# Products that nobody reads in the waits at the seams, key transposes spread over a run-up, and a reordered entry of a feed-forward

## The reference

```
x = x + tanh(g_xattn[l]) * attention_l(layernorm(x), ctx)
x = x + tanh(g_ffn[l])   * feed_forward_l(layernorm(x))
```

## Time and profile before

| | |
|---|---|
| median of the runs | 1395.36 us (3 runs, 1392.48 to 1397.9) |
| the profiled execution | 1396.31 us, of which its span is 1394.3 us |
| TensorE busy | 1329.4 us, 95% of the span |
| VectorE busy | 921.2 us, 66% |
| ScalarE busy | 604.1 us, 43% |
| GpSimd busy | 502.3 us, 36% |
| mean granted TensorE clock | 0.981 |

### The profile page before, as it was taken

How to read it: one execution, slowest core, us unless ns; L and a number is a source line. 1 busy time by engine, 2 the same in 40 slices (tenths; PEclk the granted TensorE clock), 3 DMA queues, 4 the chain that set the end, 5 groups by cost and what they waited for, 6 DMA issues and landing times.

```text
span 1394.3 us, 21141 instructions
## 1 busy us (share of the span) xinstructions
PE 1329.4 (95%) x8191; PEld 1081.1 (78%) x8191; DVE 921.2 (66%) x1352; ACT 604.1 (43%) x1046; POOL 502.3 (36%) x364
## 2 busy tenths in 40 slices
PE   6999999999999999998999999999899999899987
PEld 5989888988889889987798888889785444477733
DVE  5588778864588778875557774587756774343277
ACT  3444444443344444442244443344335778222252
POOL 5126435371126646415312543124343000243212
PEclk9999999999999999999999999999997999999989
DMA  5111111121011121020121112012104000462000
GB/s 189 54 54 50 47 52 56 31 72 39 16 54 50 46 72 42 16 94 20 27 63 55 48 37 68 22 30 61 31 1 132 2 1 2 140 156 73 1 0 31
DMA packets 55105, 70.94 MB, mean 51 GB/s; under 512 B 26672, under 2 KB 32976, under 8 KB 55008
## 3 DMA queue, kind: packets, MB, share of 16 engines
q1 hardware_dynamic: 55008, 69.60, 16.8%
HBM read 57.13 MB, written 5.37 MB: 45 GB/s over the span
## 4 chain that ended last, share of the span: by engine, by line
PE 85%; DVE 9%; ACT 3%; issue 2%; DMA 0%; POOL 0%; SPq 0%; DVEq 0%; ACTq 0%
PE ps L771 13%; PE ps L746 12%; PE ps L720 9%; PE ps L755 9%; PE ps L713 8%; PE ps L705 5%; PE ps L1709 4%; PE ps L690 4%; PE ps L1313 3%; PE ps L1339 3%; PE ps L1722 2%; PE ps L1295 1%; PE ps L1324 1%; PE ps L1414 1%; PE ps L1032 1%
## 5 line engine op out<-in xcount | busy, mean ns | idle before, releaser
L847 ACT ACTIVATE pT<-ps 128x768 fp32r<-128x768 f32 x192 | 156.0, 813 | 290.9 <-PE ps L755 289.6
L771 PE MATMUL ps<-pT,vv 128*128 128x256 f32 (+1 forms) x1728 | 251.3, 290 | 2.5 <-DVE oT L957 2.5
L950 DVE TENSOR_TENSOR pT<-ps,pT 128x768 fp32r<-128x768 f32 x192 | 183.7, 957 | 78.5 <-ACT pT L847 77.9
L746 PEld LDWEIGHTS ps<-kT,qT 128*128 128x128 f32 (+1 forms) x1152 | 201.2, 188 | 41.6 <-DVE qT L902 1.9
L746 PE MATMUL ps<-kT,qT 128*128 128x512 f32 (+3 forms) x1152 | 231.4, 336 | 1.5 <-DVE qT L902 1.5
L771 PEld LDWEIGHTS ps<-pT,vv 128*128 128x128 f32 (+1 forms) x1728 | 215.2, 180 | 3.1 <-DVE pT L950 2.9
L855 ACT ACTIVATE prob<-ps,rows_and_turned 128x768 f32<-128x768 f32 x192 | 172.5, 898 | 77.9 <-DVE rows_and_turned L938 77.9
L938 DVE TENSOR_REDUCE rows_and_turned<-ps 128x1 f32<-128x768 f32 x192 | 182.7, 951 | 24.8 <-PE ps L746 24.5
L630 POOL TENSOR_TENSOR wo<-raw,one 128x512 fp32r<-128x512 f32 (+1 forms) x48 | 50.0, 1041 | 409.9 <-PE ps L720 407.8
L720 PE MATMUL ps<-wo,oT 128*128 128x512 f32 (+1 forms) x576 | 169.0, 402 | 5.1 <-DVE x L892 2.4
L755 PE MATMUL ps<-ident,prob 128*128 128x128 f32 x1152 | 157.3, 272 | 3.0 <-DVE pT L950 3.0
(11 more groups left out here) (248 smaller groups left out, 1859.1 us busy)
## 6 DMA issues: line engine op xcount, KB each, us to landing
raw<-in_l_wq SPq DMA_DIRECT2D x44, 256.0 KB, 2.7
f2raw<-in_f_w SPq DMA_DIRECT2D x11, 776.0 KB, 4.6
rows_and_turned<-in_m_w SPq DMA_DIRECT2D x11, 768.0 KB, 4.3
raw<-in_l_wo SPq DMA_DIRECT2D x32, 256.0 KB, 2.6
raw<-in_l_wo SPq DMA_DIRECT2D x16, 192.0 KB, 2.6
w3gu<-rows_and_turned SPq DMA_DIRECT2D x11, 256.0 KB, 3.1
ctxraw<-in_ctxT SPq DMA_DIRECT2D x2, 1024.0 KB, 7.7
ctxn<-in_ctx SPq DMA_DIRECT2D x1, 2048.0 KB, 8.6
```

The costliest lines, as they stand in the source:

```text
L746: last = nc.tensor.matmul(sc[:, lo:hi], query(A, h, qp)[:, r * P:(r + 1) * P], keys(A, h // A.g)[0:hd, kp, b, lo:hi], start=(qp, kp) == PA ...
L771: last = nc.tensor.matmul(bank(6, 256, hd), vv[:, vp, b * VT + j, group % 2 * hd:(group % 2 + 1) * hd], pT[:, q % 2, pp, j, :], start=(j = ...
L847: nc.scalar.activation(turned_p(m, HI), ps[:, 4:6, 0:S // 2].rearrange("p a (j c) -> p a j c", j=3), ACT.Copy).then_inc(sem("att_pT_hi"), 1)
L950: nc.vector.tensor_tensor(turned_p(m, LO), ps[:, 4:6, 0:S // 2].rearrange("p a (j c) -> p a j c", j=3), turned_p(m, HI).bitcast(F32), ALU. ...
```

## The change

`unread_products(b, n)` issues `n` products of the 128 x 128 identity with itself into PSUM bank `b`; nothing reads them. They stand in six places: in the first attention before its second key product; around the first row transposes of the first and the second feed-forward (`turn_between`, 6 and 6 each); before the second feed-forward's second product (4); between the row transposes ahead of the third feed-forward (7, 1 and 3); between the four `f2db` products (3, 3 and 2).

The key transposes of the run-up stand at 12 of its 22 steps, on TensorE and ScalarE alike (`KEY_STEPS`: steps 1, 3, 5, 7, 9, 10, 12, 14, 16, 18, 20 and 21).

At three entries the products of the high parts come first, so that only the last ones wait for the remainder: the first attention's `K, 0, 2`, the first feed-forward's `base`, and the `f2a` product of the third feed-forward. There the zeros of banks 0 to 3 come behind the `f2a` product, ScalarE and VectorE split `f2a` earlier, VectorE turns row tile 0 ahead of normalising the last one, and the constants of the fourth attention (`consts3_dve`) are computed inside the loop.

```diff
+        def unread_products(b, n):
+
+            for _ in range(n):
+                nc.tensor.matmul(bank(b, P), ident[:], ident[:], start=True, stop=True)
...
-        def turn_between(pe, u, work):
+        def turn_between(pe, u, work, unread=0):
+            unread_products(4, unread)
             turn_row(pe, u, 0)
+            unread_products(4, unread)
             for r in range(RT):
...
+                    by_half = [(k, wp, xp) for wp, xp in ((HI, HI), (LO, HI), (HI, LO)) for k in range(KT)]
+                    products = by_half if what == A.first[1] == ("K", 0, 2) else by_tile
...
+                        if products is by_half and i == 2 * KT:
+                            pe.wait_ge(sem("xT_lo"), RT)
...
                 turn_pe(pe, u)
-                pe.wait_ge(sem("xT_lo"), RT)
+                unread_products(3, 2)
+                pe.wait_ge(sem("xT_hi"), RT)
                 job(A.first[1])
...
             def base(r):
-                pe.wait_ge(sem("f0_xT_lo"), r + 1)
-                for k in range(KT):
-                    for xp, wp in PAIRS:
+                for xp, wp in PAIRS:
+                    if xp == LO:
+                        pe.wait_ge(sem("f0_xT_lo"), r + 1)
+                    for k in range(KT):
...
-            turn_between(pe, 1, base)
+            turn_between(pe, 1, base, 6)
...
-            turn_between(pe, 3, experts)
+            turn_between(pe, 3, experts, 6)
...
             last.then_inc(sem("f1_turned"), 1)
+            unread_products(4, 4)
...
+        LATE_KEYS = 2 * G2 - 4
+        KEY_STEPS = [n for n in range(AHEAD2) if n * LATE_KEYS // AHEAD2 < (n + 1) * LATE_KEYS // AHEAD2]
...
                 score(n)
-                if n + 4 < 2 * G2:
-                    keys(n + 4)
+                if n in KEY_STEPS:
+                    keys(4 + KEY_STEPS.index(n))
...
                 add_to_x(r, 4 + r, 4, sem("added"))
-                ln_row_dve(v, 5, r, sem("added"), 2 * RT + r + 1)
+                if r < RT - 1:
+                    ln_row_dve(v, 5, r, sem("added"), 2 * RT + r + 1)
+                if r == 1:
+                    mlp2_split_dve(v)
+            ln_row_variance(v, 5, RT - 1, sem("added"), 3 * RT)
+            ln_row_out(v, 5, RT - 2)
+            turn_dve(v, 6, range(1))
+            ln_row_out(v, 5, RT - 1)
+            turn_dve(v, 6, range(1, RT))
...
+        def mlp2_turn_pe(pe):
+            turn_row(pe, 6, 0)
+            turn_row(pe, 6, 1)
+            unread_products(4, 7)
+            turn_row(pe, 6, 2)
+            unread_products(4, 1)
+            turn_row(pe, 6, 3)
+
         def mlp2_pe(pe):
+            unread_products(4, 3)
             pe.wait_ge(sem("f2_a_split"), 1)
+            nc.tensor.matmul(bank(6, 512, 16), zeros[:, 0:16], zeros[:], start=True, stop=False)
+            pe.wait_ge(sem("xT_hi"), 7 * RT)
+            for wp in (HI, LO):
+                for k in range(KT):
+                    nc.tensor.matmul(bank(7, 512, 96), f2a[:, wp, k, :], xT[:, HI, k, :], start=(wp == HI and k == 0),
+                                     stop=False)
             pe.wait_ge(sem("xT_lo"), 4 * RT)
+            for k in range(KT):
+                last = nc.tensor.matmul(bank(7, 512, 96), f2a[:, HI, k, :], xT[:, LO, k, :], start=False,
+                                        stop=(k == KT - 1))
+            last.then_inc(sem("f2_aT_full"), 1)
             for r in range(RT):
                 nc.tensor.matmul(bank(r), zeros[:, 0:P], zeros[:], start=True, stop=False)
...
                                  stop=True).then_inc(sem("f2_out"), 1)
+                unread_products(5, (3, 3, 2, 0)[r])
...
         def mlp2_act(a):
             a.wait_ge(sem("f2_a"), 16)
-            a.wait_ge(sem("layer_done"), 5)
+            a.wait_ge(sem("l2_rows"), G2)
...
                                         ALU.subtract).then_inc(sem("f2_lo"), 1)
+                if j == 1:
+                    consts3_dve(v)
...
-            turn_pe(pe, 6)
+            mlp2_turn_pe(pe)
             mlp2_pe(pe)
...
             att2_out_dve(v)
-            mlp2_split_dve(v)
-            consts3_dve(v)
-            turn_dve(v, 6)
             mlp2_dve(v)
```

19 lines of the change are left out of this document (6 added, 13 removed).

## The result

The changed kernel takes **1389.57 us** (median of 20 executions; 19 of them from 1378.93 to 1398.28) against 1397.22 for the kernel before on the same chip: ratio **0.9934**, 95% interval 0.9916 to 0.9952. The forecast was 1377.5 with a range of 1372 to 1386: the sign was right, the size was not. The profiled execution took 1389.77 us, span 1387.8.

What follows compares the result with a forecast made beforehand. TensorE, 85% of the chain, was taken to bound the kernel through its work, waits and low-clock stretches. Gains of 0.3 + 1.4 + 0.4 + 2.3 + 5.2 + 4.9 + 4.1 = 18.6 us off 1396.3 gave 1377.5, range 1372 to 1386.

Steps and rivals of the forecast that it cites:

- the fourth attention: Fourth attention, first `f2db` product to VectorE's second sum: full clock and an earlier start gain 4.1 us (0 to 4.5).
- the run-up: Third attention, first score to first turned score: spread keys take 19.5 us instead of 21.8, gaining 2.3 (1.0 to 3.3).
- the first group of the main loop: Third attention: 13.1 us instead of 18.3 if the clock is full there, gaining 5.2 (0 to 5.7).
- I place it with the former: Third attention's run-up: 0.59 us of full-width transposes in every pair of steps was taken to hold the full clock.
- the rival in which only the fourth attention loses the clock: Clock falls again in the fourth attention; its 4.1 us shrink to 0.3, total 1381.5 us; chance 0.34.
- the rival to which I gave 0.03: Spread transposes do not hold the clock: it falls early in the run-up, 10 us lost there, total 1399; chance 0.03.
- No cost: Fourth attention: `f2db` and eight unread products take 5.2 us, ready at 1327.1, before VectorE takes the result at 1328.64.
- one of the forecast's own signs of being wrong: The prediction is wrong if row transposes wait for TensorE's own unread products.
- First feed-forward: Its entry: base products at full clock, started earlier on the high parts, gain 1.4 us (0.4 to 1.6).
- Second feed-forward: Its entry: second transposes and first products at full clock shorten the tail by 0.4 us (0 to 0.7).
- Entry of the third: Third feed-forward: high parts first and one late remainder bring `gate_up` 4.9 us sooner (3.0 to 5.2).
- First attention: First key product starts sooner on the high parts; the value weights' split caps the gain at 0.3 us (0 to 0.3).

Runs made afterwards that it cites:

- the other run: The changed kernel measured once more, nothing altered, for a second profile: 1396.0 us, ratio 0.9961 against the kernel before.
- keys alone: Kernel before with the key transposes spread over the run-up and nothing else: 1400.12 us, ratio 1.0002.
- the filled kernel: Changed kernel with one unread product in each of the run-up's 10 steps without keys, none between the `f2db` products: 1384.05 us, 1384.97 when run again.
- The profile of 1414.91 us named above: Profiled execution of the kernel before with keys spread and one unread product in each thin run-up step, nothing else; that kernel's median 1393.48 us, ratio 0.9981.
- filled, with closing ones: Changed kernel with one unread product in each thin run-up step, keeping those between the `f2db` products: 1387.0 us, ratio 0.9917.
- the doubled kernel: Changed kernel with one unread product in each thin run-up step and those between the `f2db` products doubled (6, 6, 4): 1382.97 us, 1385.05 when run again.

## Why the prediction was wrong, step by step

**The steps that failed.** In the profiled execution 6.5 us came of the forecast 18.6. Of the 12 that are missing, 5.8 belong to the fourth attention (4.1 forecast, 1.7 lost), 4.3 to the run-up (2.3 forecast, 2.0 lost) and 1.6 to a low stretch that was not foreseen. In the second profile of the changed kernel the first group of the main loop is missing too (19.31 us against the 13.1 of the forecast).

**The run-up and the first group.** The step that failed is "less than in the stretch that held the clock and far more than in the one that lost it. I place it with the former." The spread run-up belongs to neither side. In four of 19 executions (and two of 11 in the other run) the mean clock of 0.996 or more leaves no room for a fall like those in the profiles (13.7 us at half the clock alone make it 0.995), so I take it that it held; they came out at 1378.9 to 1380.95 us, near the 1381.5 of the rival in which only the fourth attention loses the clock. None of the six was profiled. In both profiled executions it fell at the run-up's start, as in the rival to which I gave 0.03, and the mean clocks of the others (0.991 to 0.976) fit such a fall without showing it. That rival's price was too high (10 lost; keys alone lose 4.5 in the run-up and 1.0 in the first group in their profile). I had doubled all of TensorE's 18.9 us. But in that low stretch no score waits for VectorE, the two scores between groups of transposes run side by side, and a pair with its four transposes takes 1.77 us, so the run-up took 26.3, not 32.

What is shown: the thin steps are what lets the clock fall. In the six profiles with spread keys and empty thin steps it fell in the run-up, at 1050.6 to 1053.9; in the nine counted ones with something in each thin step (six with a product, three with a transpose) it did not. A product there kept twelve executions of twelve of the filled kernel at a mean clock of 0.994 or more, and products ahead of the run-up did not. The profile of 1414.91 us named above speaks against it: it has a filled run-up and a fall there, though only 1.3 us after its first score, so what lies ahead of the run-up may matter as well, which no run separates. The Trainium skill (TensorE: Matmul & The Clock Gate, Part 4) says that transposes do not count as busy in the same way. The runs do not settle it: a transpose in each thin step held the clock through the run-up in three profiles of three, and it takes less of TensorE than a product (0.27 us until the next score against 0.42).

**The run-up's size** was off too. I had 19.5 us for it at the full clock. At the full clock it is 21.57 with ten transposes more and 23.20 with ten products. I had let a pair of scores with its four transposes cost 1.45 and VectorE catch up over a pair. A score waits for the maximum of the last but one, and in the changed kernel's profile a pair took 1.58 with such a wait in it, 1.70 with a transpose between the scores (1050.23 to 1051.93). So the held run-up gains little over 21.8; no profile shows it held without filling. The first group was priced rightly where the clock held: 12.80 against my 13.1, a gain of 5.5 in the changed kernel's profile.

**Fourth attention: 4.1 forecast, 1.7 lost** in the profile (17.96 to 19.70), 3.3 in the second one. The step that failed is the "No cost" of the closing products together with a clock that holds ("8.7 us, 4.4 at the full one"). The clock fell at 1318.8, in the midst of the closing products. The sum had them done 5.2 us after the first; they took 7.8, and TensorE's first row transposes, which had come 5.88 us after the first closing product (1321.89 to 1327.77), came after 7.77 (1313.63 to 1321.40), behind TensorE's own products. That was one of the forecast's own signs of being wrong, and it is the whole loss: from there to the second sum it is 12.07 us before and 11.93 now, nearly all of it at the lower clock.

The price of the unread products was too low by less: a closing product alone takes 0.86 (8 records in 3.70 us are four), with three unread ones 1.92, so these cost 1.06 us instead of 0.66. Where the clock held until 1322.3 (filled, with closing ones), the first transposes came after 6.58 us and the whole stretch took 15.82, which costs nothing against none. As an estimate, these 6.58 us and the 7.73 from the first transposes to the second sum at the full clock (16.09 - 8.36 in the doubled kernel's last profile) make 14.3, near the 13.9 that the forecast had; no profile shows it. The rival for this place left 0.3 us of the gain; it didn't count that a low clock would stretch the products in TensorE's own way. (The expectations above call a closing step 0.43; that is one of the product's two records.) Why the clock falls there in some executions and not in others stays open: of the profiles with single closing products it fell 3 to 5 us behind the first one in three and 8 us behind it in the fourth.

**What held.** First feed-forward: 12.95 to 11.99, and 0.1 sooner: 1.0 of 1.4 (without the products 13.57 in one profile, where the clock fell there, and 11.99 in another, where it did not). Second feed-forward 0.3 of 0.4, from its two stretches. Entry of the third 28.69 to 23.62: 5.07 of 4.9, through the order of remainders and products (the forecast gave that 3.0 of it and the clock the rest). First attention: 0.3 forecast, nothing seen; the first value product starts at 28.35 against 28.15.

**Not foreseen:** a low stretch at 690.8 in the second attention, 1.6 us (332.11 against 330.53). It is in the profile without unread products too (332.19) and not in the second one of the changed kernel, so it comes and goes with the execution. In both profiles of the changed kernel TensorE was busy for 1.90 us of the 3.4 from 687.4 to 690.8, and only in one did the clock fall.

The sum in the profiled execution: 1.0 gained up to the first feed-forward, 1.6 lost at 690.8, 0.3 gained, 2.0 lost and 5.5 gained in the third attention, 5.1 gained, 1.7 lost: 6.6, and the two executions are 1396.3 - 1389.77 = 6.5 apart.

## What to carry to other kernels

Where thin work sits between a stretch that holds the clock and one that loses it, forecast a mixture over executions, not one of the two, and take the clock of a dozen executions before believing one profile. Place filler where the thin steps are, and measure what it costs in the chain (here 0.42 us of TensorE, against a wait of some 0.2) and in the steps beside it. Ask as well what stands behind the filler if the clock falls all the same: here the next row transposes had to wait for it. Reordering that lets products start on the part that is ready first gave its 5 us in 13 of the 17 profiles that have it (23.6 us); in the other four, where the clock was low for 3.4 us in the attention's last products, 3.4 were left (25.3).

## What the runs showed of the hardware

- A lowered clock can last while the profile counts TensorE as never idle: 41.00 us busy of 41.00, and 13.70 of 13.70. In the kernel before, low stretches of 3.4 us ended by themselves.
- The same waits do not always cost the clock. With a filled run-up and no other unread products TensorE waits 1.49 and 1.53 us ahead of the first two groups of row transposes of the first feed-forward, much as in the kernel before, where the clock fell at 636.0. Here it did not:

```profile
636.00:639.40 3.40, 2.83 (x15) 1.00 0.00 0
```

- The same program loses the clock in different places: the filled kernel's two profiles differ by a stretch of 3.4 us at 1181.1, which costs 1.7 (25.32 against 23.62), and the changed kernel's by where and how long the run-up is low.
- Six unread products of 128 columns in a row take 1.60 us (12 records from 1312.27), the last one's end included; one alone between two scores takes 0.42 until the next score starts.
- Two scores of 48 rows, which the code places in the two halves of the array's rows, run side by side: the first two of the run-up lie together in 0.51 us at the full clock (1048.89), two in 0.79 at the lower one (1057.30), as long as one.
